# Splitting Wq ahead of the third tile of rows, and normalising each tile behind its own statistics

## The reference

```python
x = x + xattn(layernorm(x), ctx, ctx, Wq, Wk, Wv, Wo)     # x: 32 x 32 x 1024, ctx: 32 x 257 x 1024
# inside: q = (layernorm(x) @ Wq)       Wq: 1024 x 1024
#         k = ctx @ Wk, v = ctx @ Wv    Wk, Wv: 1024 x 256
#         softmax(q k^T / sqrt(32)) v @ Wo, 32 heads, 8 heads of keys and values
x = x + attn(layernorm(x), eta)
x = x + ffn(layernorm(x), gate_w, expert_w)               # 2 of 8 experts per row
```

## Time and profile before

| what | value |
|---|---|
| three timed runs | 1135.96, 1136.12, 1134.29 us (median 1135.96) |
| the profiled execution | 1133.16 us |
| its span in the trace | 1131.5 us |
| TensorE matmuls busy | 1057.2 us, 93% |
| weight loads busy | 966.1 us, 85% |
| VectorE busy | 663.1 us, 59% |
| ScalarE busy | 449.7 us, 40% |
| mean granted clock of TensorE | 0.969 of full speed |

### The profile page before, as it was taken

One profiled execution on the slowest core, in us unless ns is written; L12 is line 12 of the kernel. 1 busy time (PEld: TensorE's weight loads), 2 busy tenths in 40 slices (PEclk: granted clock), 3 DMA queues, 4 the chain that ended last, 5 costly groups with the idle time before them and its releaser, 6 DMA issues. The chain is left out here.

```text
span 1131.5 us, 25873 instructions
## 1 busy us (share of the span) xinstructions
PE 1057.2 (93%) x8958; PEld 966.1 (85%) x8959; DVE 663.1 (59%) x1672; ACT 449.7 (40%) x1087; POOL 269.2 (24%) x452
## 2 busy tenths in 40 slices
PE   5799989999999999999999998699998899998993
PEld 5799889999999999999999997577766687877882
DVE  6442246666666666676666666478878355555520
ACT  2221235555555555555555555323324043333300
POOL 2000112111111111111211110044453334334432
PEclk9899999999999999999999998699999899999997
DMA  9144376756656556575665646435556667676321
GB/s 330 40 155 160 98 211 181 207 156 184 195 164 205 163 177 205 159 199 165 181 206 158 196 132 225 123 146 112 95 137 221 246 251 252 221 271 242 98 74 53
DMA packets 82744, 197.84 MB, mean 175 GB/s; under 512 B 18608, under 2 KB 29232, under 8 KB 78544
## 3 DMA queue, kind: packets, MB, share of 16 engines
q1 hardware_dynamic: 64672, 154.15, 43.9%
q0 software_dynamic: 17968, 42.29, 11.8%
HBM read 159.69 MB, written 44.56 MB: 181 GB/s over the span
## 5 line engine op out<-in xcount | busy, mean ns | idle before, releaser
L451 ACT ACTIVATE prob<-bank,nmax 128x257 f32<-128x257 f32 x256 | 122.2, 477 | 242.9 <-DVE nmax L591 242.7
L591 DVE TENSOR_REDUCE nmax<-bank 128x1 f32<-128x257 f32 x256 | 108.8, 425 | 158.2 <-PE bank L784 158.2
L671 PE MATMUL bank<-cT_h,wkv_h 128*128 128x256 f32 x512 | 155.0, 303 | 0.0
L680 PE MATMUL bank<-wkv_h,cT_h 128*128 128x256 f32 x512 | 154.4, 302 | 0.0
L671 PE MATMUL bank<-cT_h,wkv_l 128*128 128x256 f32 x512 | 145.0, 283 | 0.0
L671 PE MATMUL bank<-cT_l,wkv_h 128*128 128x256 f32 x512 | 144.7, 283 | 0.0
L680 PE MATMUL bank<-wkv_h,cT_l 128*128 128x256 f32 x512 | 144.5, 282 | 0.0
L680 PE MATMUL bank<-wkv_l,cT_h 128*128 128x256 f32 x512 | 143.9, 281 | 0.0
L344 POOL DMA_DIRECT2D qcat<-q_scratch x128 | 70.3, 555 | 270.7 <-PE bank L784 267.8
L706 PE MATMUL bank<-ident,prob 128*128 128x128 f32 x512 | 101.3, 280 | 10.5 <-DVE pT L244 7.3
L1668 PE MATMUL bank<-w_h,rows_h 128*128 x272 | 108.7, 400 | 0.0
(11 more groups left out here) (212 smaller groups left out, 2432.2 us busy)
## 6 DMA issues: line engine op xcount, KB each, us to landing
kcat<-k_scratch SPq DMA_DIRECT2D x128, 258.0 KB, 4.2
cx<-in_context SPq DMA_DIRECT2D x32, 1024.0 KB, 7.0
raw<-in_expert_w SPq DMA_DIRECT2D x48, 512.0 KB, 6.5
qcat<-q_scratch POOLq DMA_DIRECT2D x128, 128.0 KB, 3.1
k_scratch<-kT_h SPq DMA_DIRECT2D x32, 258.0 KB, 2.7
k_scratch<-kT_l SPq DMA_DIRECT2D x32, 258.0 KB, 2.9
x_in<-in_x SPq DMA_DIRECT2D x16, 512.0 KB, 6.7
expert_raw<-in_expert_w SPq DMA_DIRECT2D x16, 512.0 KB, 9.7
```

The source lines that it names most:

```text
L451: act.activation(prob[:, 1 - par, s, 0:SK], s_ps[s % 2][:, 0:SK], ACT.Exp, bias=nmax[:, 1 - par, s:s + 1], accum_out=sums[:, 1 - par, s:s ...
L591: dve.reduce_max(nmax[:, 1 - par, s:s + 1], s_ps[s % 2][:, 0:SK], AXX, negate=True).then_inc(max_done, 1)
L671: o = pe.matmul(k_ps[:, j * 256:(j + 1) * 256], wkv[w][:, k, j * P:(j + 1) * P], cT[t][:, b % 2, k, :], start=(j == 0 and k == 0 and n == ...
L680: o = pe.matmul(v_ps[:, a * KV:(a + 1) * KV], cT[t][:, b % 2, k, a * P:(a + 1) * P], wkv[w][:, k, KV:2 * KV], start=(a == 0 and k == 0 and ...
```

## The change

Four things change, none of them on TensorE:

- SyncE issues the load of the second tile of x ahead of all chunks of Wq. Before it stood behind the first chunk.
- On ScalarE each of the first two chunks of Wq is split ahead of the tile it stood behind, and chunks 2 to 7 are split in one row ahead of `x_high(2)`.
- On VectorE `normalized(0)` stands right behind `statistics(0)`, ahead of `statistics(1)`.
- On VectorE `wq_low(0)` goes ahead of `x_low(0)` and `wq_low(1)` ahead of `x_low(1)`, and chunks up to 7 go ahead of `x_low(2)`; the statistics and normalisations of tiles 2 and 3 are spread between them.

```diff
             load_x(0)
+            load_x(1)
             for c in range(KC):
                 sp.dma_start(wq_raw[:, c, :], wq[c * P:(c + 1) * P, :]).then_inc(chunk_loaded[c], 16)
-                if c == 0:
-                    load_x(1)
             load_x(2)
...
+            wq_high(0)
             x_high(0)
-            wq_high(0)
+            wq_high(1)
             x_high(1)
-            wq_high(1, 2, 3, 4)
+            wq_high(2, 3, 4, 5, 6, 7)
             x_high(2)
-            wq_high(5, 6)
             x_high(3)
-            wq_high(7)
             q_high(0, 0, 1, 2, 3)
...
             statistics(0)
+            normalized(0)
             statistics(1)
-            normalized(0)
             normalized(1)
+            wq_low(0)
             x_low(0)
-            wq_low(0)
+            wq_low(1)
             x_low(1)
-            wq_low(1, 2)
+            wq_low(2, 3)
             statistics(2)
-            wq_low(3)
+            wq_low(4)
             normalized(2)
-            wq_low(4)
+            wq_low(5)
             statistics(3)
-            wq_low(5)
+            wq_low(6)
             normalized(3)
+            wq_low(7)
             x_low(2)
-            wq_low(6)
             x_low(3)
-            wq_low(7)
             statistics(4)
```

## The result

| | before | after |
|---|---|---|
| median of six runs each | 1137.38 us | 1125.36 us |
| lowest, highest | 1134.29, 1142.39 | 1124.66, 1131.72 |
| profiled execution | 1133.16 us | 1131.72 us |
| its span | 1131.5 us | 1130.1 us |

The ratio is 0.9913, with a 95% interval of 0.9889 to 0.9937: faster by 9.9 us, between 7.2 and 12.6. (The two medians lie 12.0 us apart, but four of the six runs after stand at 1124.7 to 1125.4 and two at 1131.3 and 1131.7, so the median sits at the edge of a group.) The forecast was 8.4 us, and its 1127.5 us lies between the runs. But the two profiled executions differ by 1.4 us only. So two questions stand: where the 8.4 us were made, and where the profiles lose them.

The account below looks back on a forecast made before the run. TensorE was taken as the bound, with two early waits on Wq chunks. Waits -6.38, clock -3.00 and start +1.0 gave -8.4 us, from median 1135.96 to 1127.5 us, range about 1124.5 to 1129.5, up to 1131.0 with the first rival.

Parts of the forecast that it names:

- What bounds it: TensorE before 52.23 us: two idle gaps of 2.94 us, waiting for late Wq chunks, from the written order alone.
- The sum of the moved chunks: Third turning to first matmul of group 1: 19.76 us shrinks to 10.38, so 9.38 us go.
- Its halves: Behind the third and fourth turnings: 3.19 us wait and 1.50 us slow clock each, together 6.38 and 3.00.
- The first rival: At the two gaps: waits go but the clock still falls, 3.00 us stay; gain 5.4, 1130.6 us; chance 0.08.
- the priced stretch: TensorE from the turning at 32.47 to group 1's first matmul at 52.23: 10.38 us without gaps at 2.4 GHz.
- The start: Up to the first queries: first matmul at about 16.75 instead of 15.73, plus 1.0 us, bounds 0 to 1.9.
- The stretched normalisation: VectorE's normalized(1) beside GpSimd's memsets: kept at 1.59 us instead of 0.76, ending at 12.2.
- VectorE's later row: VectorE's work behind the moved chunks comes later; slack 3.4 and 3.8 us at tiles 4 and 5, priced at nothing.
- The slack at the first unit of group 1: x_low(3) ready before TensorE needs it: 3 us against 3.75, under 1 us of slack, but it holds.
- No slow clock in the first queries: First queries' slow matmuls, 24 before: no change priced, minus 0.8 to plus 0.8 us in the range.
- The fourth rival: First queries: clock doesn't come up after the new start; with all 192 matmuls slow +7.3, 1143.3 us; chance 0.04.
- The total: Whole kernel: 8.4 us faster, 1127.5 us, range about 1124.5 to 1129.5; forecast's chance 0.82.

Follow-up runs that it names:

- split_only: Kernel before with only chunks 5 to 7 of Wq split ahead of the third tile, start unchanged; median 1129.46 us, ratio to before 0.9917.
- one_wait: Changed kernel with chunk 7 of Wq alone back behind the fourth tile; median 1134.33 us, ratio to before 0.9961.
- filled: Kernel before plus 24 useless matmuls behind each of turn_x(2) and turn_x(3), so TensorE works through both waits; median 1135.86 us, ratio 0.9977.
- before_again: Kernel before once more, unaltered; median 1139.30 us, ratio 0.9994.
- start_only: Changed kernel with chunks 5 to 7 of Wq back behind the third and fourth tiles, new start kept; median 1139.05 us, ratio to before 0.9993.
- xlow_first: Changed kernel with x_low(0) ahead of wq_low(0) and x_low(1) ahead of wq_low(1) again; median 1129.94 us, ratio to before 0.9918.
- both: Kernel xlow_first with GpSimd's three memsets moved ahead of its first statistics work; median 1126.94 us, ratio to before 0.9892.
- best: Kernel both with statistics(1) ahead of normalized(0) again; medians 1126.16 and 1127.80 us in two groups of runs, ratios to before 0.9897 and 0.9905.

## Why the prediction was right

- **What bounds it** held: two waits made by the written order. split_only takes both away, and one_wait brings one of them back with its 2.94 us.
- **The sum of the moved chunks**, 9.38 us by the forecast: 9.25 in split_only at one count, and the stretch itself 10.36 against 10.38.
- **Its halves**, 6.38 for waits and 3.00 for the clock: filled removes the second alone and gains 2.6 to 2.8. The first rival (the clock falls all the same) is out: the priced stretch ran at 1.00. At all seven gaps of 2.94 us in four profiles (before, before_again, start_only, one_wait) the clock went to 0.50 for 3.4 us, and each fall began between 0.5 us ahead of the gap's end and 1.5 us behind it. The Trainium skill's page "TensorE: Matmul & The Clock Gate", section "HAM oscillation — how this bites in real kernels", would lay such a fall only to longer gaps. These seven contradict it.
- **The start** was forecast at +1.0 and measured at +0.57 (16.30 against 15.73). The mechanism is shown by xlow_first. The size was off by 0.45 us. Of it 0.30 are that the first tile's statistics began earlier than in the profile before (4.34 against 4.64); in all nine profiles with the new order of loads they began at 4.32 to 4.47, in the four with the old at 4.59 to 4.76, so this belongs to the change and was missing in the sum. Another 0.12 is the step from `statistics(1)` to `normalized(1)`, 2.53 us against 2.65.
- **The stretched normalisation** took 1.59 us, as kept in the sum, and both shows that it was the memsets. `wq_low(0)` began at 11.76, when they had ended (11.30), and took 1.21 us; it was not stretched. The rule of the Trainium skill's page "GPSIMD Engine Reference", section "Key points", changed nothing here, as said.
- **VectorE's later row** cost nothing: from 30 to 126 us TensorE has one wait, of 1.2 us at the turning of the first context, which before has too (at 127.8). The slack at the first unit of group 1, feared to be under 1 us, was 1.2: `x_low(3)` ended at 42.26, and the unit began at 43.44.
- **No slow clock in the first queries**: 24 slow matmuls, as before. The fourth rival is out. That count moves by itself, 16 to 27 over the profiles, worth 1.0 us.
- **The total** was hit better by the runs than by the one profile: 9.9 us against 8.4, with the interval around both. At the mark it is 8.79, which is the forecast with the start at +0.57. That the absolute time, 1127.5, came within 2.1 us of the median is in part luck: it was counted from three runs of before (median 1135.96), all six give 1137.38, and groups of runs of the changed kernel have medians from 1125.36 to 1131.26.

## What to carry to other kernels

On an engine that works in strict order, work whose data have long landed must not stand behind an instruction that waits for another engine: here three chunks of Wq behind two turnings cost 9.3 us, nearly a third of it through the clock. And a pair of changes is priced apart: one half of this one was worth 9.3 us, the other cost 0.5. With the low parts in their old order (1.1 us), the memsets in idle time (0.8) and both statistics first (1.1), the kernel stands 3.0 us ahead of the changed one at the mark, and 2.5 ahead of split_only. What the early load of the second tile is worth by itself no run here shows.

## What the hardware showed beyond that

- 48 useless matmuls in two idle gaps made the kernel faster (ratio 0.9977, 0.9962 to 0.9992), since the clock stayed up.
- Gaps of 2.94 us were followed by 3.4 us at half the clock in seven cases of seven, yet a wait of 3.37 us elsewhere in the same program (kernel best, 143 us) was not.
- GpSimd's memsets (two of 128 x 512, one of 128 x 128) stretched a `tensor_scalar` of 128 x 1024 on VectorE from 0.81 to 1.59 us. Moved away, the instruction was back at 0.81.
